# Attention output stored unnormalised; the output projection multiplies by reciprocals read back as rows

## The reference

```python
kv = concat([context, latents], axis=1)             # 4 x 1857 x 512, latents = layernorm(x)
q = rms_norm((latents @ Wq) by 32 heads, q_norm_w)  # head size 128
k = rms_norm((kv @ Wk) by 8 kv heads, k_norm_w);  v = (kv @ Wv) by 8 kv heads
probs = softmax(q @ k.T / sqrt(128))                # 4 query heads share one kv head
out = (probs @ v) heads side by side, @ Wo          # 4 x 256 x 4096, times 4096 x 512
x = x + tanh(g_xattn) * out
x = x + tanh(g_ffn) * ffn(layernorm(x))
```

## Time and profile before

| | |
|---|---|
| median of 3 executions | 3195.52 us (3192.04 to 3196.73) |
| the profiled execution | 3194.47 us, span 3191.4 us |
| PE busy | 3006.7 us, 94% |
| DVE busy | 2464.5 us, 77% |
| ACT busy | 2051.1 us, 64% |
| POOL busy | 1329.4 us, 42% |
| granted TensorE clock, mean | 0.972 of full speed |
| attend, from its first tiles to its last store | about 257 to 2714 us |
| project | about 2715 to 2921 us |

### The profile page before, as it was taken

One profiled execution on the slowest core, in us unless ns is written; L12 is line 12 of the kernel. 1 busy time (PEld: TensorE's weight loads), 2 busy tenths in 40 slices (PEclk: granted clock), 3 DMA queues, 4 the chain that ended last, 5 costly groups with the idle time before them and its releaser, 6 DMA issues. The chain is left out here.

```text
span 3191.4 us, 51782 instructions
## 1 busy us (share of the span) xinstructions
PE 3006.7 (94%) x14650; PEld 2447.2 (77%) x14650; DVE 2464.5 (77%) x3317; ACT 2051.1 (64%) x2899; POOL 1329.4 (42%) x791
## 2 busy tenths in 40 slices
PE   6995999999899999998999999999999997797899
PEld 5884788888678888886788888778888885585677
DVE  6773888888968888887788888868888888413765
ACT  3443777777857778876787777767787886311211
POOL 1330455555525555554355555535555555000000
PEclk9997999999999999998999999999999998898899
DMA  6973101011211100102111110210010000734200
GB/s 229 276 232 115 37 34 39 33 37 46 75 35 34 45 33 33 35 34 85 34 34 43 36 36 33 73 51 31 33 48 34 33 27 10 228 94 135 91 30 20
DMA packets 183907, 210.87 MB, mean 66 GB/s; under 512 B 10964, under 2 KB 125652, under 8 KB 182760
## 3 DMA queue, kind: packets, MB, share of 16 engines
q1 hardware_dynamic: 179016, 196.27, 19.0%
q0 software_dynamic: 2176, 8.39, 0.8%
q10 hardware_dynamic: 2592, 4.72, 0.5%
HBM read 140.14 MB, written 69.21 MB: 66 GB/s over the span
## 5 line engine op out<-in xcount | busy, mean ns | idle before, releaser
L873 POOL TENSOR_TENSOR att_sm<-att_sm,att_sc 128x1024 f32<-128x1024 f32 (+1 forms) x384 | 854.3, 2225 | 675.1 <-DVE att_pr L824 674.7
L679 PE MATMUL att_ppv<-att_pr,att_V 128*128 128x512 f32 (+1 forms) x2880 | 849.8, 404 | 25.6 <-DVE att_pr L824 22.9
L659 PE MATMUL att_pqk<-att_q,att_kT 128*128 128x512 f32 (+1 forms) x2880 | 850.8, 405 | 6.1 <-issue 3.1
L751 ACT ACTIVATE att_sc<-att_pqk,att_rk 128x512 f32<-128x512 f32 (+1 forms) x960 | 661.1, 689 | 184.4 <-PE att_pqk L659 181.8
L620 PE MATMUL att_pkv<-att_ctxT,att_wkv 128*128 128x512 f32 (+1 forms) x3072 | 762.2, 378 | 1.1 <-DVE att_kT L840 0.5
L824 DVE TENSOR_TENSOR att_pr<-att_sc,att_pr 128x1024 fp32r<-128x1024 f32 (+1 forms) x512 | 643.9, 1258 | 39.2 <-ACT att_pr L762 39.1
L620 PEld LDWEIGHTS att_pkv<-att_ctxT,att_wkv 128*128 128x128 f32 x3072 | 564.8, 191 | 121.7 <-DVE att_kT L840 1.2
L679 PEld LDWEIGHTS att_ppv<-att_pr,att_V 128*128 128x128 f32 (+1 forms) x2880 | 533.4, 191 | 153.4 <-DVE att_pr L824 39.5
L659 PEld LDWEIGHTS att_pqk<-att_q,att_kT 128*128 128x128 f32 (+1 forms) x2880 | 506.1, 185 | 121.8 <-ACT att_sc L751 14.3
L818 DVE TENSOR_TENSOR att_sc<-att_sc,att_pmax 128x1024 f32<-128x1024 f32 (+1 forms) x512 | 585.0, 1143 | 16.9 <-PE att_pmax L628 16.8
L762 ACT CAST att_pr<-att_sc 128x1024 fp32r<-128x1024 f32 (+1 forms) x512 | 510.4, 997 | 113.0 <-PE att_ppv L679 111.5
(11 more groups left out here) (131 smaller groups left out, 2687.4 us busy)
## 6 DMA issues: line engine op xcount, KB each, us to landing
q_scr<-pre_qT SPq DMA_DIRECT2D x128, 256.0 KB, 3.5
att_wkv<-kv_scr SPq DMA_DIRECT2D x64, 512.0 KB, 3.9
att_q<-q_scr SPq DMA_DIRECT2D x64, 512.0 KB, 4.2
o_scr<-att_on SPq DMA_DIRECT2D x64, 256.0 KB, 2.0
out_oraw<-o_scr SPq DMA_DIRECT2D x64, 256.0 KB, 4.7
att_sc<-in_ctx SPq DMA_DIRECT2D x16, 768.0 KB, 4.9
pre_wq_raw<-in_L_xattn_Wq SPq DMA_DIRECT2D x8, 1024.0 KB, 7.2
kv_scr<-pre_kv SPq DMA_DIRECT2D x8, 1024.0 KB, 7.7
```

Of the source, the lines that this page charges most:

```text
L659: mm = pe.matmul(pqk[0:m, (h * NT + t) % 2], kT[:, kp, t * P:t * P + m], q[:, qp, h], start=(i == 0), stop=(i == 2))
L679: mm = pe.matmul(ppv[:], V[0:m, vp, t], pr[0:m, pp, (t // 2) % NP, t % 2], start=(t == 0 and i == 0), stop=(t == NT - 1 and i == 2))
L751: act.activation(sc[0:m, h, t], pqk[0:m, s % 2], ACT.Copy, scale=rk[0:m, t:t + 1]).then_inc(sc_ok, 1)
L873: pool.tensor_tensor(sm[0:m, 0:w], sm[0:m, 0:w], sc[0:m, h, i:i + w], ALU.add).then_inc(sum_ok, w)
```

## The change

In `attend`, `db` and `on` are gone. ACT copies `pv`'s result to one of two `oraw` buffers, and `st` stores that. `rden` has two buffers too, and a new step `ds` stores it to a new scratch tensor `rd_scr`, 128 x 4 elements of 4 bytes. `mt` and the very last `dt` wait for `den_ok` in place of `on_ok`. The numbers of all tables are new.

In `project`, every load of a tile is four DMAs in place of two: beside each 256 KB of `o_scr` one that reads the reciprocals of four heads as rows of 512 bytes and repeats them on all 128 partitions, 256 KB again, to `rdb`, which has two slots. DVE multiplies `oraw` by `rdb` in place ahead of ACT's `HI`. DVE's loop is now one step staggered: the product of tile `v`, then the `LO` of tile `v - 1`. The wait ahead of a load is `olo_ok >= b * NV + v - 1`. The residual goes in place into `xin`, which is loaded later.

```diff
+        rd=nc.dram_tensor("rd_scr", [B * KVH, G, S], F32, kind="Internal").ap(),
...
-        rden = sb("rden", [P, 4])
-        oraw = sb("oraw", [P, HALF])
-        on = sb("on", [P, HALF])
+        rden = sb("rden", [P, NH, 4])
+        oraw = sb("oraw", [P, NH, HALF])
...
-        TILE = dict(copy=0.39, pv=24.5, sub=19.4, exp=21.0, hi=21.7, lo=22.4, sum=23.0, max=0.98)
-        END = dict(mt=(2.79, 0.69),
...
-                   oraw=(23.4, 23.1),
-                   fold=(24.8, 23.1),
-                   dt=(24.67, 24.47),
-                   dred=(28.43, 26.63),
-                   db=(31.76, 40.56),
-                   on=(30.61, 30.51),
-                   st=(28.31, 28.31),
+        TILE = dict(copy=0.29, pv=24.4, sub=19.5, exp=21.0, hi=21.6, lo=22.3, sum=23.6, max=1.18)
+        END = dict(mt=(2.29, 0.79),
+                   red=(1.7, 4.0),
+                   mb=(5.2, 5.3),
+                   oraw=(23.6, 23.1),
+                   fold=(24.8, 25.3),
+                   dt=(24.37, 24.37),
+                   dred=(30.23, 29.53),
+                   ds=(31.23, 29.13),
+                   st=(23.9, 22.5),
                    ldq=(-29.9, -29.9))
...
-        LOADS = dict(ldwk=-26.5, ldwv=-11.4)
+        CHUNK = (dict(k=(-12.28, -12.16, -11.1), v=(-1.66, -0.9, -0.18), khi=-9.76, klo=-10.23, kn=-6.56, var=-7.76, pow=-2.26, vhi=-1.66, vt=15.7, vthi=15.36, vtlo=15.34),
...
+        LOADS = dict(ldwk=-26.6, ldwv=-6.0)
...
+                    elif what == "ds":
+                        sp.wait_ge(rden_ok, AHEAD + NH * n + h + 1)
+                        sp.dma_start(scr["rd"][bass.ds(n, 1), h * G // NH:(h + 1) * G // NH]
+                                     .rearrange("o g (c p) -> p (o g c)", p=P), rden[:, h],
+                                     allow_slow_non_contiguous=True).then_inc(rd_out[h], 16)
                     elif what == "st":
-                        sp.wait_ge(on_ok, AHEAD + NH * n + h + 1)
+                        sp.wait_ge(oraw_ok, AHEAD + NH * n + h + 1)
                         sp.dma_start(scr["o"][bass.ds(n, 1), :, h * G // NH:(h + 1) * G // NH]
-                                     .rearrange("o p g s -> (o p) (g s)"), on[:]).then_inc(o_out, 16)
+                                     .rearrange("o p g s -> (o p) (g s)"), oraw[:, h]).then_inc(o_out[h], 16)
 
                 rounds(sp, step)
-                sp.wait_ge(o_out, AHEAD + 16 * NH * B * KVH)
+                for h in range(NH):
+                    sp.wait_ge(o_out[h], AHEAD + 16 * B * KVH)
+                    sp.wait_ge(rd_out[h], AHEAD + 16 * B * KVH)
...
                     elif what == "mt":
                         pe.wait_ge(max_ok, AHEAD + maxima(u, NT - 1))
-                        pe.wait_ge(on_ok, AHEAD + u - 1)
+                        pe.wait_ge(den_ok, AHEAD + u - 1)
...
                         if last and h == 1:
-                            pe.wait_ge(on_ok, AHEAD + u)
+                            pe.wait_ge(den_ok, AHEAD + u)
...
-                    elif what == "db":
-                        pe.wait_ge(rden_ok, AHEAD + u + 1)
-                        spread(pred, rden, ident).then_inc(db_ps, 1)
...
                     elif what == "oraw":
                         act.wait_ge(pv_ps, AHEAD + NT * (u + 1))
-                        act.wait_ge(on_ok, AHEAD + u)
-                        act.copy(oraw[:], ppv[:]).then_inc(oraw_ok, 1)
+                        act.wait_ge(o_out[h], AHEAD + 16 * n)
+                        act.copy(oraw[:, h], ppv[:]).then_inc(oraw_ok, 1)
...
-                        dve.wait_ge(db_ps, AHEAD + u)
-                        dve.reciprocal(rden[:], den[:]).then_inc(rden_ok, 1)
-                    elif what == "on":
-                        dve.wait_ge(db_ps, AHEAD + u + 1)
-                        dve.wait_ge(oraw_ok, AHEAD + u + 1)
-                        dve.wait_ge(o_out, AHEAD + 16 * u)
-                        dve.tensor_tensor(on[:], oraw[:], pred[:], ALU.mult).then_inc(on_ok, 1)
+                        dve.wait_ge(rd_out[h], AHEAD + 16 * n)
+                        dve.reciprocal(rden[:, h], den[:]).then_inc(rden_ok, 1)
...
-        x2 = sb("x2", [P, BT, D])
+        rdb = sb("rdb", [P, 2, HC, P])
...
                 steps = [(2 * v - 6, "load", v // BT, v % BT) for v in range(NV)]
-                steps += [(-1.5, "x", 0, t) for t in range(BT)] + [(2 * NV + 1 + t, "store", 0, t) for t in range(BT)]
+                steps += [(3.2 + t, "x", 0, t) for t in range(BT)] + [(2 * NV + 1 + t, "store", 0, t) for t in range(BT)]
 
                 def step(b, what, e, t):
                     v = e * BT + t
                     if what == "load":
-                        sp.wait_ge(olo_ok, AHEAD + b * NV + (v + 1) - SL)
+                        sp.wait_ge(olo_ok, AHEAD + b * NV + v - 1)
                         for k in range(HC // G):
                             sp.dma_start(oraw[:, v % SL, k * G:(k + 1) * G],
                                          scr["o"][bass.ds(b * KVH + (e * (HC // G) + k), 1), :, :, t * P:(t + 1) * P]
                                          .rearrange("o p g s -> (o p) g s")).then_inc(o_in[v % SL], 16)
+                            sp.dma_start(rdb[:, v % 2, k * G:(k + 1) * G],
+                                         scr["rd"][bass.ds(b * KVH + (e * (HC // G) + k), 1), :, t * P:(t + 1) * P]
+                                         .rearrange("o g s -> (o g) s").partition_broadcast(P)).then_inc(o_in[v % SL], 16)
...
                     elif what == "x":
-                        sp.wait_ge(x2_ok, AHEAD + b * BT + t - 1)
+                        sp.wait_ge(x2_out[t], AHEAD + 16 * b)
...
                     elif what == "store":
                         sp.wait_ge(x2_ok, AHEAD + b * BT + t + 1)
-                        sp.dma_start(scr["x2"][bass.ds((b * BT + t) * P, P)], x2[:, t]).then_inc(x2_out[t], 16)
+                        sp.dma_start(scr["x2"][bass.ds((b * BT + t) * P, P)], xin[:, t]).then_inc(x2_out[t], 16)
...
-                            act.wait_ge(o_in[v % SL], AHEAD + (b * (NV // SL) + v // SL + 1) * (16 * HC // G))
+                            act.wait_ge(on_ok, AHEAD + b * NV + v + 1)
                             act.wait_ge(o_ps, AHEAD + b * NV + (v + 1) - SL)
                             act.copy(o[:, v % SL, HI], oraw[:, v % SL]).then_inc(ohi_ok, 1)
...
-                    for e in range(NE):
-                        for t in range(BT):
-                            v = e * BT + t
-                            dve.wait_ge(ohi_ok, AHEAD + b * NV + v + 1)
-                            dve.tensor_tensor(o[:, v % SL, LO], oraw[:, v % SL], o[:, v % SL, HI].bitcast(F32),
+                    for v in range(NV + 1):
+                        if v < NV:
+                            dve.wait_ge(o_in[v % SL], AHEAD + (b * (NV // SL) + v // SL + 1) * (32 * HC // G))
+                            dve.tensor_tensor(oraw[:, v % SL], oraw[:, v % SL], rdb[:, v % 2], ALU.mult).then_inc(on_ok, 1)
+                        if v >= 1:
+                            z = v - 1
+                            dve.wait_ge(ohi_ok, AHEAD + b * NV + z + 1)
+                            dve.tensor_tensor(o[:, z % SL, LO], oraw[:, z % SL], o[:, z % SL, HI].bitcast(F32),
                                               ALU.subtract).then_inc(olo_ok, 1)
                             if first:
-                                dve.wait_ge(whi_ok, v + 1)
-                                dve.tensor_tensor(wo[:, LO, WC * v:WC * v + WC], wraw[:, v % 2],
-                                                  wo[:, HI, WC * v:WC * v + WC].bitcast(F32), ALU.subtract).then_inc(wlo_ok, 1)
+                                dve.wait_ge(whi_ok, z + 1)
+                                dve.tensor_tensor(wo[:, LO, WC * z:WC * z + WC], wraw[:, z % 2],
+                                                  wo[:, HI, WC * z:WC * z + WC].bitcast(F32), ALU.subtract).then_inc(wlo_ok, 1)
...
                     for t in range(BT):
                         dve.wait_ge(o_ps, AHEAD + b * NV + NV - BT + t + 1)
                         dve.wait_ge(x_in[t], AHEAD + 16 * b + 16)
-                        dve.wait_ge(x2_out[t], AHEAD + 16 * b)
-                        dve.scalar_tensor_tensor(out=x2[:, t], in0=po[:, t], scalar=gcol[:, 1:2], in1=xin[:, t],
+                        dve.scalar_tensor_tensor(out=xin[:, t], in0=po[:, t], scalar=gcol[:, 1:2], in1=xin[:, t],
                                                  op0=ALU.mult, op1=ALU.add).then_inc(x2_ok, 1)
```

More of the change, by code:

```diff
@@ L426, in attend @@
                  "qk_ps sc_ok max_ok mt_ps red_ok mb_ps sub_ok exp_ok phi_ok plo_ok sum_ok pv_ps oraw_ok "
-                 "dt_ps den_ok rden_ok db_ps on_ok fold_ok").split()
+                 "dt_ps den_ok rden_ok fold_ok").split()
         loop_sems = [sem(n) for n in names]
@@ L920, in project @@
         x_in, x2_out = [sem("x_in0"), sem("x_in1")], [sem("x2_out0"), sem("x2_out1")]
-        whi_ok, wlo_ok, ohi_ok, olo_ok, o_ps, x2_ok = (
```

(3 more changed lines are left out.)

18 lines of the change are left out of this document (8 added, 10 removed).

## The result

The median is 3263.26 us (3252.91 to 3267.53, 4 executions) against 3194.86 (3192.04 to 3196.73, 4 executions) of the kernel before: a ratio of 1.0215, 95% interval 1.0197 to 1.0233. The change makes the kernel 68 us slower. The forecast was 30 us slower, in a range up to 3275.

A forecast was written before the change was run, and what follows sets the result against it. PE was taken as the bound, in project giving way to serial loads: 54.9 (later batches) + 27.7 (first) + 8 (clock) - 61.6 (attend) = +29.0 us, from 3194.5 to 3223.5, shown as a 3225 median; range 3194 to 3275.

The forecast's parts named there:

- The cycle: In project, closed from LO through load and product to LO: 8.41 us a tile, bounds 7.81 and 8.91; PE needs 5.44.
- The later batches: In project, three batches at 65.7 us against 47.41: 54.9 us more, between 44 and 64.
- The first batch: In project, first tiles and Wo pieces land first, then six slower cycles of 10.41 us: 27.7 us more, 24 to 37.
- The clock: In project, PE's idling lowers its clock to 0.8, showing only in each batch's last two tiles: 8 us more, 0 to 20.
- Rival 3: In project, the clock falls to its lower level for the cycles, a tile taking 10.88 us: +61, 3286 us; chance 0.12.
- attend: Stage sum from PE's shorter work, a shorter wait and an earlier last store: 61.6 us less, bounds 52 to 75.
- the wait for `on`: In attend, mt's 8.2 us wait for on, now for the earlier den_ok, half counted: 4 us less.
- I cost it at nothing: In attend, the new store ds delays no loads: DMA is little busy and loads are issued many tile steps ahead; zero.
- the tail: At attend's end, the last store is issued 2.8 us earlier: 1.5 us of gain, between 3 and -1.
- 1: attend returns more than project costs, closing half of PE's 65.5 us of idling: -27, 3168 us; chance 0.10.
- 2: In project, the loads are not serialised and only each batch's start costs: 3143 us; chance 0.04.
- 4: In project, reading the same rows for 128 partitions is slow, adding 48 us over 24 cycles: 3273 us; chance 0.12.

The follow-up runs named there:

- the kernel with the wait for the product: Changed kernel with SP's wait ahead of load v in project for the product of tile v - 2, not its LO: 3185.45 us, ratio 0.9979.
- the plain rows: Changed kernel loading rdb from o_scr, 256 KB at 128 different places, in place of two rows repeated for all partitions: 3275.35 us, ratio 1.0255.

## Why the prediction was right in kind and short in size

**The cycle** was the right mechanism: PE waits for `LO` at each tile of the cycle, and starts of products are 8.8 to 9.8 us apart. The mis-sized term is the landing of the fourth DMA. I took 3.9 us, the mean of a pair's 3.3 and a row of 4.4, plus 0.1 to DVE; it measured 4.65. SP's four issues took 2.08, not 1.9. 9.22 against 8.41 is 0.8 a cycle, 4.9 a batch. Over the 18 cycles it ran from 3.97 to 5.12, so my upper bound of 4.4 was too low. The figure of 4.4 is a median over four loads out of ten that SP issued in a row, not over four from an idle queue, and the cycle waits for the last of its four: in the one that starts at 2859.68 they land 3.2, 4.1, 4.4 and 4.9 us behind their issues. The Trainium skill's 6.15 us for a load of 1 MB ("DMA: Bandwidth & Descriptors", Measured), which I set beside the sum as 8.76 a cycle, was nearer, though short too. Issue and landing together measured 6.7.

**The later batches** came to 71.3 us on average where 65.7 was forecast. In the third: 4.3 from the residual to the first `LO`'s end (3.5 forecast), six cycles of 9.27 = 55.6 (50.5), and 11.3 for the last two tiles and the residual (11.7). One batch of before was also 45.8 us where I took 47.41 for all three. Together 18.5 us over the term of 54.9.

**The first batch**, +29.3 for +27.7: right in sum, and by luck. Its cycles measured 10.13 us, forecast 10.41, but that is 0.9 above the later ones where I had added 2.0 for the pieces of `Wo`, on a base that was 0.8 too short. The first `LO` ended 19.1 us into the stage and not 16.7.

**The clock.** I added 8 us. The clock did fall, to a mean of 0.88 of full speed over the later batches, and it went back and forth between its two levels, 1.2 and 2.4 GHz. PE's timeline of after, two neighbouring tiles:

```profile
2850.51 8.54 PE L1030 MATMUL out_po<-out_wo,out_o 128*128 128x512 f32 x24 [4.39 <-DVE out_o L1003]
2859.55 5.74 PE L1030 MATMUL out_po<-out_wo,out_o 128*128 128x512 f32 x24 [0.50 <-DVE out_o L1003]
```

Two stretches of 1 us while PE works on the first of them (columns as in the earlier trace rows, the clock third from the end):

```profile
2855.50:2856.50 1.00, 1.00 (x4) 0.81 (x3) 0.00 (x0) 0.00 (x0) 0.00 (x0) 0.50 0.83 246
2857.50:2858.50 1.00, 1.00 (x6) 0.81 (x5) 1.00 (x2) 0.04 (x1) 0.00 (x0) 1.00 0.00 0
```

The first tile, behind an idling of 4.39 us, has its first 6 us at 0.50 and takes 8.54 us; the second, behind 0.50 us of idling, is at 1.00 throughout and takes 5.74. All tiles of the cycles, at most 8.54 us, fit into a cycle of 9.2, and the last two tiles took no longer than forecast without a clock term. Rival 3 had the lower level for whole cycles; it came for parts of some, and did not show in the time. The oscillation that the Trainium skill describes ("TensorE: Matmul & The Clock Gate", HAM oscillation) was there, down to the lower level of 0.50; here the wait for the loads was longer than what it cost. The 2.7 us of the rest need not belong to it: in the kernels without the cycle the rest measured 270.1 to 273.9 us, and 273.2 in after lies among them.

**attend** is the larger error: 34.6 us for 61.6. By its terms:

- `db` off PE: 56.1 forecast; PE is busy 53.9 less, 2322.4 to 2268.5, up to the last reciprocal. Right.
- the wait for `on`: +4 forecast. PE's idling in the stage rose instead, from 64.5 to 78.7: -14.2. "The waits may only move to the next step in line" is what happened (6.1 us for the maximum). The rest is the step that failed: "I cost it at nothing", said of the store `ds`, with DMA's low share as the cover. (A tile step is nearer 2.5 us than the 2.3 of that cover; nothing hangs on it.) With 128 pieces for 512 the idling is 67.1. So 11.6 of the 14.2 are the 4-byte pieces; the 2.6 left are less than the same kernel's executions differ by. The cover held for bytes and not for pieces: with 2 KB more a half the DMA share went from 0.12 to 0.17, and to 0.13 with 16-byte pieces.
- the tail: +1.5 forecast, -5.0 measured, outside my bounds of 3 and -1. The store was issued as early as I said, and landed 8.1 us later or more (the last three: median 10.3), where a store of 256 KB takes 2.0. With 16-byte pieces the tail is 3.6 us and not 11.7, 3.1 less than before. Its landing "isn't shown by any row", and I took the nearest row, a store with long runs.

Errors of 27.0 in `attend`, 18.5 in the later batches, 1.6 in the first and 2.7 in the rest, less the 8 for a clock that cost nothing, make 41.8, against the 70.7 - 29.0 = 41.7 by which the span was missed.

**Rivals.** 1: `attend` returned less, not more. 2: refuted, the loads were serial; the kernel with the wait for the product is what it described, and is 3185 and not 3143 us. By the span of its profiled execution, one of its faster ones, the miss is 38 us: 26 in `attend`, 9 in the first batch (76.1 against 64.7 + 2.3) and 3 in the later ones. 4: refuted by the plain rows. The closed cycle is the whole of the sign: with either of its two parts taken out the change is a gain of 0.2 to 0.4%, with both in place a loss of 2%.
